# Experts of a decoder layer: two of four dense passes replaced by passes over tokens sorted by expert

## The reference, cut to what matters

```python
B, S, D, F, E = (4, 256, 128, 256, 8)      # TOP_K = 2, LOOPS = 2
z = _rmsnorm(y, norm_w)                    # y: what the loop before left
gates = softmax(z @ router_w)              # the two largest, rescaled to sum 1
y = y + sum over the two chosen experts e of gates[e] * (silu(z @ w1[e]) * (z @ w3[e])) @ w2[e]
```

## Time and profile before

| | |
|---|---|
| median of 3 runs | 591.04 us (590.68 to 594.41) |
| span of the profiled execution, first to last instruction | 589.0 us |
| TensorE busy | 517.7 us (88%) |
| VectorE busy | 454.7 us (77%) |
| ScalarE busy | 281.6 us (48%) |
| GpSimd busy | 168.4 us (29%) |
| mean granted TensorE clock | 0.954 of full speed |

### The profile page before, as it was taken

One profiled execution on the slowest core, in us unless ns is written; L12 is line 12 of the kernel. 1 busy time (PEld: TensorE's weight loads), 2 busy tenths in 40 slices (PEclk: granted clock), 3 DMA queues, 4 the chain that ended last, 5 costly groups with the idle time before them and its releaser, 6 DMA issues.

```text
span 589.0 us, 9198 instructions
## 1 busy us (share of the span) xinstructions
PE 517.7 (88%) x3231; PEld 301.3 (51%) x3231; DVE 454.7 (77%) x1172; ACT 281.6 (48%) x493; POOL 168.4 (29%) x129
## 2 busy tenths in 40 slices
PE   7798999999999999999999954565669999999866
PEld 5344766665666666666665610121223565666423
DVE  6799857765783367676455789999999689999896
ACT  4640465555542244243233345655540377777655
POOL 8623000000000000020000015999994145554030
PEclk9999999999998999999999995778879999999989
DMA  5000430000100000100000000000000100000001
GB/s 136 27 16 0 152 99 3 1 1 3 45 1 0 1 1 1 37 5 2 0 1 0 2 0 0 0 1 1 0 0 0 46 2 1 2 3 1 2 0 37
DMA packets 10769, 9.27 MB, mean 16 GB/s; under 512 B 2050, under 2 KB 9540, under 8 KB 10724
## 3 DMA queue, kind: packets, MB, share of 16 engines
q1 hardware_dynamic: 10724, 8.69, 5.2%
HBM read 6.98 MB, written 0.52 MB: 13 GB/s over the span
## 4 chain that ended last, share of the span: by engine, by line
PE 63%; DVE 29%; ACT 4%; issue 3%; POOL 1%; DVEq 0%; POOLq 0%; ACTq 0%
PE PS L1221 19%; PE PS L759 10%; PE PS L1247 9%; DVE PS L1790 6%; DVE VA L1803 5%; PE PS L821 5%; PE PS L804 5%; DVE PS L1796 3%; PE PS L779 2%; PE PS L831 1%; PE PS L735 1%; PE PS L472 1%; DVE sums L585 1%; DVE E L581 1%; DVE XN L268 1%
## 5 line engine op out<-in xcount | busy, mean ns | idle before, releaser
L1221 PE MATMUL PS<-XNT,KSA 128*128 128x512 f32 x256 | 121.7, 609 | 0.0
L804 PE MATMUL PS<-QM,KP 32*128 32x256 f32 x512 | 91.8, 398 | 1.2 <-ACT E L992 0.8
L1229 ACT ACTIVATE E<-PS 128x512 f32<-128x512 f32 x64 | 38.1, 597 | 108.6 <-PE PS L1221 108.3
L1235 DVE TENSOR_TENSOR E<-E,PS 128x512 f32<-128x512 f32 x64 | 43.9, 687 | 58.6 <-ACT E L1229 57.3
L759 PE MATMUL PS<-KP,QP 32*128 32x256 f32 x512 | 78.0, 400 | 0.5 <-ACT QP L970 0.5
L992 ACT ACTIVATE E<-PS 128x512 f32<-128x512 f32 x100 | 56.1, 595 | 34.9 <-PE PS L804 24.3
L1247 PEld LDWEIGHTS PS<-KSA,E 128*128 128x128 f32 x512 | 62.4, 192 | 16.9 <-issue 15.7
L1221 PEld LDWEIGHTS PS<-XNT,KSA 128*128 128x128 f32 x256 | 46.2, 195 | 42.7 <-issue 42.5
L804 PEld LDWEIGHTS PS<-QM,KP 32*128 32x128 f32 x512 | 60.5, 184 | 6.2 <-issue 4.8
L309 PE MATMUL PS<-KSA,select 128*128 128x512 bf16 x64 | 25.8, 495 | 42.4 <-ACT KSA L1687 30.7
L1247 PE MATMUL PS<-KSA,E 128*128 128x128 f32 x512 | 62.4, 275 | 0.4 <-DVE XN L1456 0.4
(11 more groups left out here) (289 smaller groups left out, 906.1 us busy)
## 6 DMA issues: line engine op xcount, KB each, us to landing
KSA<-in_w SPq DMA_DIRECT2D x2, 1024.0 KB, 6.6
X<-in_x SPq DMA_DIRECT2D x2, 256.0 KB, 3.4
SCR<-in_ctxT SPq DMA_DIRECT2D x1, 512.0 KB, 6.0
KP<-OT SPq DMA_DIRECT2D x16, 32.0 KB
SCR<-in_fside SPq DMA_DIRECT2D x1, 512.0 KB, 4.6
KP<-QM SPq DMA_DIRECT2D x16, 32.0 KB
out_x<-X SPq DMA_DIRECT2D x8, 64.0 KB, 1.5
wx<-in_w_x SPq DMA_DIRECT2D x1, 384.0 KB, 7.0
```

The costliest lines, as they stand in the source:

```text
L804: ins = pe.matmul(o[:, kt * S:(kt + 1) * S], KP[rows(i), g, t:t + P], QM[rows(i), g, b * S:(b + 1) * S], start=True, stop=True, skip_group ...
L1221: ins = pe.matmul(bank(2 * (g % 3) + o), w[:, e, c * P:(c + 1) * P], XNT[:, tokens_of(p)], start=True, stop=True)
L1229: act.activation(E6[:, 4 + g % 2, :], bank(2 * (g % 3)), ACT.Silu).then_inc(sig("silu"), 1)
L1235: dve.tensor_tensor(E6[:, g % 4, :], E6[:, 4 + g % 2, :], bank(2 * (g % 3) + 1), ALU.mult)\
```

## The change

Passes 0 and 3 stay dense. In passes 1 and 2 each token is computed only for its two experts. `pass_rank` also notes who is first and second (`top`), `pass_count` counts by 8 small bf16 matmuls how many earlier tokens chose each expert, and `pass_route` turns that into a place for each of the 1024 (token, expert) pairs, each expert beginning at a multiple of 128: 1024 / 128 + 7 = 15 tiles are always enough. GpSimd's `sort_tokens` scatters the rows of ZN into a DRAM buffer by 8 indirect transfers of 128 rows of 512 bytes; SP's `load_sorted` reads the buffer back in three loads. `pass_route` also writes for each tile where its expert's weights begin; TensorE loads these 15 numbers into registers (`expert_starts`), and the three weights of an expert now lie side by side so that one address reaches them.

A tile is `tile_up` (one matmul, 128 tokens as weights, 512 moving columns: w1 and w3), `tile_silu` and `tile_gated` on 256 columns, `turn_tile` (two transposes, since the tokens now stand on the partitions), `take_hidden` by ScalarE, and `tile_down` (two matmuls of 128 columns). VectorE copies the answers of two tiles (`take_answers`), SP stores them to DRAM (`store_answers`), GpSimd's `gather_answers` fetches the two rows of each token by 8 indirect transfers, and `mix_sorted` adds them with their gates. The two sorted passes run as 30 tiles in one loop. The roots of passes 2 and 3 move to GpSimd (`pass_power`), so ScalarE loads no table among the tiles. Side steps keep their order but get new places; the first turn and logits in pass 0 are one unit earlier. At the start two DMAs fill the sorted buffers with zeros, and sixteen weight loads share one semaphore, which each user awaits in full.

The diff, cut to its core ("..." for what is left out):

```diff
+SLOT_TILES = 2 * HALF // P + NE - 1
+SLOTS = SLOT_TILES * P
...
+        SORTED = [nc.dram_tensor("sorted_%d" % k, (SLOTS, D), F32, kind="Internal").ap() for k in range(2)]
+        ANSWERS = [nc.dram_tensor("answers_%d" % k, (SLOTS, D), F32, kind="Internal").ap() for k in range(2)]
...
+        XL = [QPf[:, k * SLOTS:(k + 1) * SLOTS].rearrange("p (t d) -> p t d", d=D) for k in range(2)]
+        XT = [QMf[:, T + k * HALF:T + (k + 1) * HALF] for k in range(2)]
+        SG = [QMf[:, 2 * T + k * FE:2 * T + (k + 1) * FE] for k in range(2)]
+        HD = [QMf[:, 2 * T + HALF + k * FE:2 * T + HALF + (k + 1) * FE] for k in range(2)]
+        HDT = [QMf[:, 3 * T + k * FE:3 * T + (k + 1) * FE] for k in range(2)]
+        YB = OTf[:, 2 * T:2 * T + SLOTS].rearrange("p (t d) -> p t d", d=D)
+        GB = OTf[:, 0:T].rearrange("p (c d) -> p c d", d=D)
...
+        DENSE = (0, 3)
...
+        TILES = 2 * SLOT_TILES
+        LOADS = (slice(0, 4), slice(4, 8), slice(8, 12), slice(12, SLOT_TILES))
+        PAIRS = (SLOT_TILES + 1) // 2
...
+            for g in range(3, UPS):
                 unit_up(pe, g)
                 if g % 2 == 1:
-                    down((g - 3) // 2)
-                if p + 1 < PASSES and n == 6:
-                    pass_turn(pe, p + 1)
-                if p + 1 < PASSES and n == 8:
-                    pass_logits(pe, p + 1)
-                if p == 0 and n in HALVES:
-                    context_half_tensor(pe, HALVES.index(n))
-                if p == 1 and n in HALVES:
-                    keys_half_tensor(pe, HALVES.index(n))
-                if p == 1 and n == 14:
+                    down(pe, (g - 3) // 2)
+                if g == 5:
+                    pass_turn(pe, 1)
+                if g == 7:
+                    pass_logits(pe, 1)
+                if g == 8:
+                    pass_count(pe, 0)
+                if g in HALVES:
+                    context_half_tensor(pe, HALVES.index(g))
+            tiles_tensor(pe)
...
+            def turn_sorted(x):
+                k, q = divmod(x, 4)
+                pe.wait_ge(sig("sorted_in_%d" % min(q, 2)), 16 * (k + 1) + (0 if q else 16 * 2))
+                if x:
+                    pe.wait_ge(sig("sorted_taken"), x)
+                else:
+                    pe.wait_ge(sig("gated"), unit_step(UPS - 2))
+                for n, t in enumerate(range(LOADS[q].start, LOADS[q].stop)):
+                    ins = pe.transpose(bank(5)[:, n * P:(n + 1) * P], XL[k][:, t, :], ident[:, :])
+                ins.then_inc(sig("sorted_turned"), 1)
+            def expert_starts(k):
+                pe.wait_ge(sig("routed"), ROUTED["experts", k])
+                _, starts = nc.values_load_multi_w_load_instructions(
+                    expert_at[0:1, k, :], engines=[mybir.EngineType.PE], min_val=0, max_val=(NE - 1) * EXPERT_WIDTH,
+                    skip_runtime_bounds_check_because="the table is clamped to the last expert before it is written")
+                return starts
+            def tile_up(i):
+                t = i % SLOT_TILES
+                pe.wait_ge(sig("sorted_taken"), load_of(i) + 1)
+                if i >= 3:
+                    pe.wait_ge(sig("gated"), tile_step(i - 3))
+                else:
+                    pe.wait_ge(sig("gated"), unit_step((UPS - 3, UPS - 1, UPS - 1)[i]))
+                pe.matmul(tile_bank(i), XT[load_of(i) % 2][:, (t % 4) * P:(t % 4 + 1) * P],
+                          WE[:, bass.ds(starts[t], 2 * FE)], start=True, stop=True).then_inc(sig("up"), 1)
+            def turn_tile(i):
+                pe.wait_ge(sig("gated"), tile_step(i))
+                if i >= 1:
+                    pe.wait_ge(sig("hidden_taken"), i)
+                for c in range(2):
+                    ins = pe.transpose(hidden_bank(i)[:, c * P:(c + 1) * P], HD[i % 2][:, c * P:(c + 1) * P], ident[:, :])
+                ins.then_inc(sig("hidden_turned"), 1)
+            def tile_down(i, start):
+                q = pair_of(i)
+                pe.wait_ge(sig("hidden_taken"), i + 1)
+                if i == 0:
+                    pe.wait_ge(sig("mixed"), mix_step(NE - 1))
+                if q >= 2:
+                    pe.wait_ge(sig("mixed"), take_step(q - 2))
+                n = i % SLOT_TILES % 2
+                for c in range(2):
+                    ins = pe.matmul(answer_columns(q)[:, n * P:(n + 1) * P], HDT[i % 2][:, c * P:(c + 1) * P],
+                                    WE[:, bass.ds(start + (2 * FE + c * P), D)], start=(c == 0), stop=(c == 1))
+                ins.then_inc(sig("down"), 1)
+            starts, older = expert_starts(0), None
+            turn_sorted(0)
+            for i in range(TILES):
+                t = i % SLOT_TILES
+                if i == SLOT_TILES:
+                    older, starts = starts, expert_starts(1)
+                tile_up(i)
+                if i == 0:
+                    down(pe, NE - 1)
+                if i >= 1:
+                    turn_tile(i - 1)
+                if i >= 2:
+                    tile_down(i - 2, starts[t - 2] if t >= 2 else older[t - 2])
+                if t % 4 == 1:
+                    if load_of(i) % 4 < 3:
+                        turn_sorted(load_of(i) + 1)
+                if i == SLOT_TILES - 1:
+                    turn_sorted(4)
+                if i == 2:
+                    pass_turn(pe, 2)
+                if i == 4:
+                    pass_logits(pe, 2)
+                if i == 5:
+                    pass_count(pe, 1)
+                if i in KEY_HALVES:
+                    keys_half_tensor(pe, KEY_HALVES.index(i))
+                if i == 12:
                     pe.wait_ge(sig("keys"), 2)
                     pe.wait_ge(sig("w_sums"), 1)
                     pe.matmul(bank(7)[:, 0:2], onesf, wscale[:, :], start=True, stop=True).then_inc(sig("w_total"), 1)
-                if p == 3 and n == 10:
-                    pe.wait_ge(sig("logits_read"), 4)
-                    half_turn(pe, 0, 7)
-                if p == 3 and n == 12:
-                    scan_steps_in(pe, 0, SCAN_BANK[0][0])
-                if p == 3 and n == 13:
-                    scan_rows_in(pe, 0, SCAN_BANK[0][1])
-                if p == 3 and n == 15:
-                    scan_delta_in(pe, 0, SCAN_BANK[0][2])
-            down(UNITS_MOE // 2 - 1)
+                if i == 27:
+                    pass_turn(pe, 3)
+                if i == 29:
+                    pass_logits(pe, 3)
+            unit_up(pe, UPS)
+            turn_tile(TILES - 1)
+            tile_down(TILES - 2, starts[SLOT_TILES - 2])
+            unit_up(pe, UPS + 1)
+            tile_down(TILES - 1, starts[SLOT_TILES - 1])
+            unit_up(pe, UPS + 2)
...
+            take_sorted(0)
+            for i in range(TILES):
+                t = i % SLOT_TILES
+                tile_silu(i)
+                if i >= 1:
+                    take_hidden(i - 1)
+                if t % 4 == 2:
+                    if load_of(i) % 4 < 3:
+                        take_sorted(load_of(i) + 1)
+                if i == SLOT_TILES - 1:
+                    take_sorted(4)
+                if i == 3:
+                    pass_scalar(act, 2)
+                if i in KEY_HALVES:
+                    keys_half_scalar(act, KEY_HALVES.index(i))
+                if i == 28:
+                    pass_scalar(act, 3)
+            take_hidden(TILES - 1)
...
+        def mix_sorted(dve, ch, k):
+            s = tiles_of(k + 1)
+            dve.wait_ge(sig("gathered"), 16 * 8 * (k + 1))
+            for c in range(2):
+                for t in range(4):
+                    j, r = s.start + t, 4 * c + t
+                    ins = dve.scalar_tensor_tensor(XN[:, j, :], GB[:, r, :], gate_of[:, k, r:r + 1], XN[:, j, :],
+                                                   ALU.mult, ALU.add)
...
+                if g == 7:
+                    pass_shift(dve, ch, 1)
+                    pass_rank(dve, ch, 1)
+                if g == 8:
+                    pass_route(dve, ch, 0)
+                if g == 10:
+                    pass_share(dve, ch, 1)
+                    pass_pick(dve, ch, 0)
...
+            for i in range(TILES):
+                tile_gated(i)
+                if i >= 2 and ends_pair(i - 2):
+                    take_answers(pair_of(i - 2))
+                if i == 0:
+                    mix(NE - 1)
+                    pass_stats(dve, ch, 2)
+                if i == 1:
+                    pass_norm(dve, ch, 2)
+                if i == 4:
+                    pass_shift(dve, ch, 2)
+                    pass_rank(dve, ch, 2)
+                if i == 5:
+                    pass_route(dve, ch, 1)
+                if i == 9:
                     feed_weight_sums(dve, ch)
-                if p == 1 and n == 15:
+                if i == 16:
                     feed_weights(dve, ch)
-                if p == 3 and n == 5:
+                if i == SORTED_MIX_AT:
+                    mix_sorted(dve, ch, 0)
```

(76 more changed lines are left out.)

415 lines of the change are left out of this document (299 added, 116 removed).

## The result

The changed kernel takes 601.92 us (median of four runs, 600.25 to 603.63) against 591.25 before, a ratio of 1.017 [1.013, 1.021]: 1.7% slower, where I had forecast 0.6% faster. The profiled execution has a span of 598.5 us against 589.0. Between equal landmarks, the 9.5 us arise so: 1.7 ahead of the experts' stage (its first matmul starts at 149.99 instead of 148.25), 6.0 in the stage (its last down ends at 345.20, 195.2 us after the start, instead of 189.2), and 1.7 behind it. TensorE's work did shrink as forecast; the stage didn't.

A forecast was written before the change was run, and what follows sets the result against it. TensorE's work was taken to bound the experts' stage: 33.1 us less work, 27.6 more waits, net -5.5; with a 1.8 us clock fall -3.7, so 591.04 becomes 587.3 us. Range 577 to 601, likeliest case 583 to 591.

The forecast's parts named there:

- What covers the DRAM detour: Scatters and gathers on GpSimd: taken at 1.04 us each, covered up to limits of 1.47 to 2.5 us each.
- mix_sorted(0) waits for gathered: Sign that the forecast is wrong: at tile 24 the first mix waits for the gathers; the first gather fits up to 1.47 us each.
- turn_sorted(4) waits for the sort: Sign that the forecast is wrong: the second sorted pass's start waits for the sort, not for SP's order (forecast wait 3.1 us).
- a granted clock below 0.9 over the tiles: Sign that the forecast is wrong: TensorE's granted clock falls below 0.9 during the 30 tiles.
- B: Rival, chance 0.17: slow index transfers decide from 1.47 us each; 596.5 us at 2.0 each, 605.0 at 2.35.
- C: Rival, chance 0.10: the ring between engines sets the tile's pace, 0.4 us a tile instead of 0.13; 595.4 us.
- A: Rival, chance 0.28: smaller waits, with no register cost, tile gap, address cost or clock fall; 8.8 us less, 578.5 us.
- Clock: One fall of TensorE's clock, at the wait before tile 15 with the copy behind it: 1.8 us.
- undisturbed tile: Each of the 30 tiles: bound by TensorE's 1.53 us of work, plus 0.13 for gap and addresses.
- second 15 registers: Second sorted pass's start: loading 15 registers in TensorE's queue, 0.1 us each, 1.5 us.
- tiles 24 and 25: Waits for the sorted mix, statistics, root and normalisation: 2.5 and 1.2 us, sum 3.7.
- gaps and addresses at each tile: All 30 tiles: 0.1 us each after a late gate (3.0) and 0.03 each for dynamic addresses (1.0), 4.0 us.

The follow-up runs named there:

- e1: Changed kernel with all 32 index transfers made plain transfers of the same size to or from fixed rows: 588.13 us, ratio 0.9934 to the kernel before.
- e6: Changed kernel with each scatter and gather waiting until the one before it has landed: 614.70 us, ratio 1.0382 to the kernel before.
- e10: On e7, a wait for the landings after every second index transfer: 597.95 us, ratio 1.0103 to the kernel before.
- e7: Changed kernel with the second sorted load issued after three stores and one register load per tile: 598.43 us, ratio 1.0090 to the kernel before.
- e17: Changed kernel with pause after each train's fourth transfer, early second load, one register load per tile, key rows and zeros later: 585.38 us, ratio 0.9888.
- e14: Kernel before, all passes dense, plus four trains of eight index gathers that nobody reads, one per pass: 592.66 us, ratio 1.0025.
- e18: e17 with the 32 index transfers made plain ones to fixed rows, without pause: 585.22 us, ratio 0.9880 to the kernel before.

## Why the prediction was wrong

**The step that failed** is "What covers the DRAM detour". It priced an index transfer as occupied time on GpSimd, 1.04 us (measured: 0.96 busy and 0.30 between two, 1.26 apart), compared that with when each result is needed, and found it covered; that comparison held. What it left out is that a train of them can slow an engine that has nothing to do with it. Nothing in the trace of before has an index transfer, and I bounded its duration but not its effect on others. By e1 this is 0.9934 against 1.0171, 14 us. That e1 comes so near to the forecast (587.3 is 0.9937 of 591.04) is partly luck. In its profile TensorE's idle time in the stage is 21.2 us more than before, where I had 27.6; falls of the clock cost 5.1 us more than before, where I had 1.8; and 1.4 us arise ahead of the stage and 2.7 behind it, where I had nothing. My list of signs was incomplete in the same way: "mix_sorted(0) waits for gathered" and "turn_sorted(4) waits for the sort" did not occur. The one that did, a granted clock below 0.9 over the tiles (0.87), does not name a cause.

**Rivals.** B named the right instructions, but its mechanism (pace over 1.47 us) isn't what happened in the change; e6 and e10 show that mechanism. C is out: undisturbed tiles are 1.53 us apart (silu at 276.26, 277.79). A was half right: there was no gap at a tile and no cost of the first registers, but the second registers cost 2.35 us and the clock fell more often, not less.

**Clock.** I priced one fall, 1.8 us. The tiles of the change had 24 us at 1.2 GHz, five periods behind idle times; two follow the late signals, one (6.8 us long) the load and the registers. On the other hand the halves with one-row matmuls kept 2.4 GHz here (TensorE's unit at 185.36 is busy 1.98 instead of 3.64), which I had left as before: two falls less, some 3 us in favour of the change in this execution, and not in that of e1. The stages of single profiles differ by such falls, so the verdicts above rest on the timed runs.

**The terms.**

| term | forecast | measured in the changed kernel |
|---|---|---|
| undisturbed tile | 1.53 + 0.13 | 1.53 |
| pass 0, turn and count | 1.7, 1.8 | 1.07, 1.50 |
| first 15 registers | 1.5 | 0 (1.77, hidden) |
| ScalarE's first copy | 0.9 | 0.86 |
| tiles 0 and 1 | 1.3, 1.6 | 1.08, 1.61 |
| second routing | 1.2, 1.4 | 1.02, 1.13 |
| second load | 3.1 | 2.33 |
| second 15 registers | 1.5 | 2.35 (3.21 of idle in all, less 0.86 that e7 keeps) |
| feed_weights | 1.5 | 1.21 |
| tiles 24 and 25 | 2.5, 1.2 | 2.36, 2.70 |
| last pass | 4.1 | 2.6, of which 0.98 behind a late signal |
| clock | 1.8 | 8.5 (half of 23.9 us at 1.2 GHz in the stage, less half of 6.8 before) |
| late signals | none | 2.53 and 5.80 on TensorE, and the 0.98 |

TensorE's idle time in the stage grew from 0.8 us, where I had read 1.7, to 31.1: 30.3 more (forecast 27.6). With the clock's 8.5 and the 33.1 of work saved the stage should be 5.7 us longer; it is 6.0.

The waits placed by hand were right to some tenths. Per register I took 0.1 us; by the rows it is 0.12 in the first table and 0.24 in the second. Why the second is twice the first I can't say. The section of the Trainium skill that the prediction cited (Runtime: NRT & Kernel Launch, Instruction fetch mechanics) gives about 0.2; where the load was not hidden, the trace is nearer to it than to my 0.1. The 4.0 us for gaps and addresses at each tile were too much.

At tile 25, where TensorE was idle 1.5 us more than forecast, stands something that I had passed over: GpSimd's other work, moved behind the gathers, now stands beside the last pass's normalisation. From the timeline of all engines:
```profile
284.93 2.87 POOL L2729 TENSOR_SCALAR OT<-SCR 128x1024 f32<-128x1024 uint8 x1
285.09 0.90 DVE L271 TENSOR_SCALAR rt<-rt 128x4 f32<-128x4 f32 x1
287.02 0.86 DVE L1824 TENSOR_TENSOR QM<-QM,PS 128x256 f32<-128x256 f32 x1
```
L271 lasts 0.17 elsewhere in the stage and L1824 0.42; with L269 and one part of L1644 four instructions of VectorE are 2.4 us longer here. It is the same in e1 and e17. Before, GpSimd's piece ran at 251.57 beside other instructions of VectorE, and none was longer. No run moves it, so what it costs in time isn't shown.

**Outside the stage.** 1.7 us arise ahead of it: mostly the fall at 22 us, which by e14 and e18 doesn't hang on the change. Of the 1.7 behind the stage, 0.9 is VectorE: the last mix starts 1.05 us after the last down, behind four operations of the state-space branch, instead of 0.11.

## What to carry to other kernels

Price a new kind of transfer twice: what it occupies, and what it does to the engines around it; if no trace has one, put a train of it into the existing kernel first, as e14 does, and look at when the other engines start, not only at the time: e14 took 0.25% more, and its time alone would not have warned of 2.4%. Break long trains of index transfers with a wait for the landings; here four at a time, since fewer made the trains themselves too long. The shorter the steps that engines hand to each other, the more a late signal costs: of 3.1 us on VectorE a chain three units deep let 0.98 through to TensorE, one of small tiles let through 2.53 of 3.0 and all of 5.8.
